# Delta attention inside a four-stage kernel: the rate products between the groups, the norm earlier, the output product between the queries, one activation table

## The reference, cut to what matters

```
xn = (x - mu) / sqrt(var + eps) * ln_w + ln_b
q, k, v = xn @ Wq.T, xn @ Wk.T, xn @ Wv.T
alpha = sigmoid(xn @ Wa.T + ba);  aR = sigmoid(xn @ WaR.T + baR)
beta  = sigmoid(xn @ Wb.T + bb);  gamma = sigmoid(xn @ Wg.T + bg)
kn = k_t / max(norm(k_t), 1e-12)
pred = S^T kn;  r = clip(v_t - pred, -1, 1)
S = a_t * S;  S = S + b_t * kn (v_t - kn S);   o  = S^T q_t
R = aR_t * R; R = R + g_t * kn (r - kn R);     o += R^T q_t
out = o @ Wo.T + residual
```

## Time and profile before

| | |
|---|---|
| time, median of 3 runs | 3872.45 us (3866.7 to 3881.83) |
| span of the profiled execution | 3870.2 us |
| TensorE matmul busy | 3279.9 us, 85% |
| TensorE weight load busy | 2481.9 us, 64% |
| VectorE busy | 2586.4 us, 67% |
| ScalarE busy | 1461.8 us, 38% |
| GpSimd busy | 942.3 us, 24% |
| ScalarE table loads of L1313 and L1371 | 32 and 31, 1283 ns each |

### The profile page before, as it was taken

How to read it: one execution, slowest core, us unless ns; L and a number is a source line. 1 busy time by engine, 2 the same in 40 slices (tenths; PEclk the granted TensorE clock), 3 DMA queues, 4 the chain that set the end, 5 groups by cost and what they waited for, 6 DMA issues and landing times. The chain is left out here.

```text
span 3870.2 us, 141857 instructions
## 1 busy us (share of the span) xinstructions
PE 3279.9 (85%) x62854; PEld 2481.9 (64%) x62854; DVE 2586.4 (67%) x5676; ACT 1461.8 (38%) x3298; POOL 942.3 (24%) x1051
## 2 busy tenths in 40 slices
PE   7775999994889988888888988888888899857888
PEld 4555999993566666666666666666666666534555
DVE  6872111212777787778777887777777877747887
ACT  2221222221454445444544454445444544421111
POOL 2333222221222222322222222222222222212110
PEclk9886999996899999999999999999999999978999
DMA  2117666662000000000000000000000000010000
GB/s 67 58 47 237 184 183 183 191 181 91 5 7 10 9 7 7 10 9 7 7 10 9 7 7 10 9 7 7 10 9 7 7 9 8 5 40 18 22 24 14
DMA packets 98175, 168.18 MB, mean 43 GB/s; under 512 B 15400, under 2 KB 71976, under 8 KB 97312
## 3 DMA queue, kind: packets, MB, share of 16 engines
q1 hardware_dynamic: 76976, 136.07, 10.6%
q0 software_dynamic: 19440, 21.97, 4.0%
q10 hardware_dynamic: 1152, 1.06, 0.1%
HBM read 118.86 MB, written 38.09 MB: 41 GB/s over the span
## 5 line engine op out<-in xcount | busy, mean ns | idle before, releaser
L1357 ACT COPY da_Ub<-da_U 32x256 f32<-32x256 f32 x1024 | 412.0, 402 | 17.1
L1051 POOL TENSOR_TENSOR da_M<-da_M,da_decay 128x512 f32<-128x512 f32 x256 | 283.4, 1131 | 456.9 <-DVE da_M L1212 322.7
L1189 DVE TENSOR_TENSOR da_eGn<-da_eGn,da_z 128x30 f32<-128x30 f32 (+14 forms) x960 | 353.6, 368 | 33.0
L1188 DVE TENSOR_TENSOR da_z<-da_eGn 128x30 f32<-128x30 f32 (+14 forms) x960 | 349.5, 364 | 27.6
L1644 PE MATMUL da_C<-da_Ub,da_Km 128*64 128x256 f32 x2048 | 313.4, 426 | 16.1 <-ACT da_Ub L1357 5.7
L829 PEld LDWEIGHTS le_ps_qkv<-le_scr,le_up 128*128 128x128 f32 x2272 | 266.0, 193 | 4.8 <-ACT le_scr L659 1.8
L829 PE MATMUL le_ps_qkv<-le_scr,le_up 128*128 128x128 f32 x2272 | 268.0, 277 | 1.2 <-ACT le_scr L659 1.2
L1476 PE MATMUL da_unit<-da_wx,da_xnT 128*128 128x512 f32 x512 | 258.1, 629 | 2.9 <-ACT da_xnT L1302 1.9
L1483 PE MATMUL da_unit<-da_xnT,da_wx 128*128 128x128 f32 x2048 | 244.4, 278 | 10.6 <-ACT da_eGn L1342 10.5
L1212 DVE TENSOR_TENSOR da_M<-da_C,da_M 128x512 f32<-128x512 f32 x256 | 176.5, 689 | 113.9 <-PE da_C L1644 108.2
L1483 PEld LDWEIGHTS da_unit<-da_xnT,da_wx 128*128 128x128 f32 x2048 | 235.7, 193 | 18.2 <-ACT da_eGn L1342 18.2
(11 more groups left out here) (303 smaller groups left out, 7105.3 us busy)
## 6 DMA issues: line engine op xcount, KB each, us to landing
le_up<-in_upT SPq DMA_DIRECT2D x71, 1024.0 KB, 5.1
le_scr<-moe_slots SPq DMA_DIRECT2D x71, 129.0 KB, 4.2
le_down<-in_downT SPq DMA_DIRECT2D x8, 1024.0 KB, 12.4
le_x<-in_x SPq DMA_DIRECT2D x16, 256.0 KB, 3.6
moe_acc<-le_y SPq DMA_DIRECT2D x32, 128.0 KB, 2.3
da_x<-moe_acc SPq DMA_DIRECT2D x128, 32.0 KB, 1.9
stream<-da_xz SPq DMA_DIRECT2D x128, 32.0 KB, 1.6
stream<-da_y POOLq DMA_DIRECT2D x128, 32.0 KB, 3.0
```

Of the source, the lines that this page charges most:

```text
L1051: ins = nc.gpsimd.tensor_tensor(st_, st_, decay[:, par, rec, 2 * g:2 * g + 2].rearrange("p a b -> p (a b)").unsqueeze(2).to_broadcast([P, ...
L1188: c.link(tt(t, Xm[:, s + 1:C, s:s + 1].to_broadcast([P, below, s]), Xm[:, s:s + 1, 0:s].to_broadcast([P, below, s]), ALU.mult))
L1189: c.link(tt(Xm[:, s + 1:C, 0:s], Xm[:, s + 1:C, 0:s], t, ALU.add))
L1357: ins = nc.scalar.copy(Ub[rows_of(b), :, :, b, :], U[rows_of(b), rec])
```

## The change

- `exponents_next` and its semaphore are gone. ScalarE loads one table with exponential and logarithm at the stage's start.
- TensorE: `turn_x` goes behind the state rows of group 1, `rates` 0 ahead of the first Gram product, `rates` 1 to where `result` was, `rates` 2 behind the state rows of group 3, `rates` 3 ahead of the predicted product of group 3. `result` goes between the two halves of the queries. `turned_outputs` 0 goes behind the second token product of group 2 (`state_update(i, 2, 0)`), `turned_outputs` 1 between the inner outputs. `turned_keys` 1 and the first half of the values go ahead of `state_update(i, 3, 0)`, `turned_keys` 2 ahead of the last inner outputs.
- VectorE: `norm_second` goes ahead of `clipped` 0, `norm_last` ahead of the gates, the four `add_bias` into groups 1, 1, 2 and 3.
- ScalarE: the copy of x, the exponentials and the logarithms are spread over groups 0 to 3 in the same way; each logarithm is by itself.
- The banks of `rates` and `turned_outputs` and the waits that guard them change with it.

No product, copy or elementwise step is added; only the small exponential of L1371 is left out.

```diff
-        RATE_BANK = (2, 0, 1, 2)
+        RATE_BANK = (0, 2, 1, 2)
+        OUT_BANK = (2, 0, 0, 0)
...
@@ VectorE, period @@
                     products(n, pn, 0, 1)
+                if norm:
+                    norm_second(i + 2)
                 if state:
                     clipped(i, par, 0)
...
                     update(i, 0, 0)
                 if norm:
-                    norm_second(i + 2)
+                    norm_last(i + 2)
                 if prepare:
                     gates(n)
...
                     products(n, pn, 1, 1)
+                if norm:
+                    add_bias(i + 2, 0)
+                if prepare:
                     gram_out(n, pn, 2)
...
                     update(i, 1, 1)
+                if norm:
+                    add_bias(i + 2, 1)
                 if prepare:
                     gram_out(n, pn, 3)
                     decays(pn, 0)
                     decays(pn, 1)
-                if norm:
-                    norm_last(i + 2)
...
                     update(i, 2, 1)
+                if norm:
+                    add_bias(i + 2, 2)
                 if prepare:
                     substitute(6, 11)
                 if state:
                     clipped(i, par, 3)
                 if norm:
-                    add_bias(i + 2, 0)
-                    add_bias(i + 2, 1)
+                    add_bias(i + 2, 3)
@@ ScalarE @@
-            def exponents_next(n):
-                need(act, warmed, n)
-                nc.scalar.activation(spare[:], mhalf[:], ACT.Exp).then_inc(warmed, 1)
...
                     queries(n, 0)
+                if put:
+                    result(i - 1)
+                if prepare:
                     queries(n, 1)
...
                 if norm:
                     copy_xT(i + 2, par)
                 if state:
+                    solved(i, 1, 0)
+                if norm:
+                    rate_exp(i + 2, 0)
+                if state:
+                    solved(i, 1, 1)
+                    outputs(i, 1)
+                if norm:
+                    rate_exp(i + 2, 1)
+                    rate_log(i + 2, 0)
+                if state:
+                    solved(i, 2, 0)
+                    turned_outputs(i, 0)
+                    solved(i, 2, 1)
+                    turned_outputs(i, 1)
+                    outputs(i, 2)
+                if prepare:
+                    turned_keys(n, 0)
+                if norm:
+                    rate_exp(i + 2, 2)
+                if state:
                     turned_outputs(i, 2)
                     solved(i, 3, 0)
+                if prepare:
+                    turned_keys(n, 1)
                 if norm:
-                    for u in range(3):
-                        rate_exp(i + 2, u)
+                    rate_exp(i + 2, 3)
+                if prepare:
+                    values(n, 0)
                 if state:
                     solved(i, 3, 1)
                 if norm:
-                    rate_exp(i + 2, 3)
...
+                    rate_log(i + 2, 1)
+                if prepare:
+                    turned_keys(n, 2)
                 if state:
                     outputs(i, 3)
                 if prepare:
                     values(n, 1)
-                    turned_keys(n, 2)
-                if norm:
-                    exponents_next(i + 1)
 
             act.wait_ge(loaded, 16 * LOADS)
+            nc.scalar.preload_act_table_set("natural_log_exp_and_others")
@@ TensorE, rates @@
                     need(pe, xT_ready, n + 1)
-                    need(pe, km_ready, (n - 1) * NG + 1)
+                    need(pe, g_ready, (n - 1) * 6 + 6)
                 elif u == 1:
-                    need(pe, oT_ready, (n - 2) * NG + 3)
-                elif u == 3:
-                    need(pe, a_ready, n * 4 + 1)
+                    need(pe, gram_done, once(n - 1, 0))
+                elif u == 2:
+                    need(pe, gram_done, once(n - 1, 3))
+                else:
+                    need(pe, a_ready, n * 4 + 2)
+                    need(pe, km_ready, once(n - 1, 0))
@@ TensorE, gram @@
                     if k == 1:
                         need(pe, g_ready, n * 6 + 6)
-                        need(pe, out_ready, n - 1)
-                    elif k == 2:
-                        need(pe, oT_ready, (n - 1) * NG + 1)
+                    if k < 3 and exists(n + 1):
+                        need(pe, a_ready, (n + 1) * 4 + k)
@@ TensorE, period @@
                     queries(n, pn, 0)
+                if put:
+                    result(i - 1)
+                if prepare:
                     queries(n, pn, 1)
...
                     state_rows(i, par, 1)
+                if norm:
+                    turn_x(i + 2)
+                if state:
                     state_update(i, 0, 1)
                     state_predicted(i, par, 1)
                     solve(i, 1, 0)
                     state_outputs(i, par, 1)
+                if norm:
+                    rates(i + 2, par, 0)
                 if prepare:
                     gram(n, pn, 2)
                 if state:
                     inner_predicted(i, par, 1)
                     state_update(i, 1, 0)
-                if put:
-                    result(i - 1)
+                if norm:
+                    rates(i + 2, par, 1)
                 if state:
                     solve(i, 1, 1)
                     inner_outputs(i, par, 1, 0)
                 if prepare:
                     gram(n, pn, 3)
                 if state:
-                    turned_outputs(i, 0)
...
                     state_update(i, 2, 0)
-                    turned_outputs(i, 1)
+                    turned_outputs(i, 0)
                     solve(i, 2, 1)
                     inner_outputs(i, par, 2, 0)
+                    turned_outputs(i, 1)
                     inner_outputs(i, par, 2, 1)
                     state_rows(i, par, 3)
+                if norm:
+                    rates(i + 2, par, 2)
                 if prepare:
                     turned_keys(n, 0)
...
-                if norm:
-                    turn_x(i + 2)
-                if state:
                     turned_outputs(i, 2)
                     solve(i, 3, 0)
                     state_outputs(i, par, 3)
                 if norm:
-                    rates(i + 2, par, 0)
+                    rates(i + 2, par, 3)
                 if state:
                     inner_predicted(i, par, 3)
-                if norm:
-                    rates(i + 2, par, 1)
+                if prepare:
+                    turned_keys(n, 1)
+                    values(n, pn, 0)
                 if state:
                     state_update(i, 3, 0)
-                if norm:
-                    rates(i + 2, par, 2)
-                if state:
                     solve(i, 3, 1)
                     inner_outputs(i, par, 3, 0)
-                if norm:
-                    rates(i + 2, par, 3)
-                if prepare:
-                    turned_keys(n, 1)
-                    values(n, pn, 0)
+                if prepare:
+                    turned_keys(n, 2)
                 if state:
                     inner_outputs(i, par, 3, 1)
```

More of the change, by code:

```diff
@@ L942, in chunked_delta @@
          tt_ready, chain, pool_chain, cleared, w_psum, w_ready, u_psum, u_ready, ub_ready, p_psum, wr_ready, ds_psum, s_updated, dr_psum, r_updated,
-         o_psum, o_ready, scaled, oT_psum, oT_ready, out_psum, out_ready, added, warmed) = [m.sem(n) for n in names]
+         o_psum, o_ready, scaled, oT_psum, oT_ready, out_psum, out_ready, added) = [m.sem(n) for n in names]
         sq = eG[:, 1, 0:DI].rearrange("p (h t) -> p h t", t=P)
@@ L1308, in rate_exp, with rate_log @@
                 nc.scalar.activation(a, a, ACT.Exp, scale=-1.0).then_inc(e_done, 1)
-            def rate_log(n):
-                for rec in range(2):
-                    need(act, e_done, n * 4 + 2 * rec + 2)
-                    nc.scalar.activation(sp[:, rec], sp[:, rec], ACT.Ln, bias=1.0).then_inc(sp_ready, 1)
+            def rate_log(n, rec):
+                need(act, e_done, n * 4 + 2 * rec + 2)
+                nc.scalar.activation(sp[:, rec], sp[:, rec], ACT.Ln, bias=1.0).then_inc(sp_ready, 1)
             def keys(n, half):
@@ L1405, in period @@
                     outputs(i, 0)
-                    solved(i, 1, 0)
-                if put:
-                    result(i - 1)
-                if state:
-                    solved(i, 1, 1)
-                    turned_outputs(i, 0)
-                    outputs(i, 1)
-                    solved(i, 2, 0)
-                    turned_outputs(i, 1)
-                    solved(i, 2, 1)
-                if prepare:
-                    turned_keys(n, 0)
-                if state:
-                    outputs(i, 2)
                 if norm:
@@ L1460, in turn_x @@
                 need(pe, xn_ready, n + 1)
-                need(pe, gram_done, once(n - 1, 3))
+                need(pe, g_ready, (n - 1) * 6 + 5)
```

(43 more changed lines are left out.)

20 lines of the change are left out of this document (6 added, 14 removed).

## The result

The changed kernel takes 3742.16 us (median of 4 runs, 3736.06 to 3752.39) where the kernel before takes 3877.14 in the same comparison: a ratio of 0.9658, 95% interval 0.9639 to 0.9677. It is faster by 3.4%, 135 us; 3759 was predicted. The profiled execution spans 3742.7 us, 127.5 less than that of before.

The account below looks back on a forecast made before the run. TensorE was taken as the bound. Removed waits of 3.7 us, less 1.4 new, plus 1.3 clock, gave 3.6 a period over 30 periods; with start and end 113 us off 3870.2, plus 2.3: 3759 us, range 3675 to 3835.

Parts of the forecast that it names:

- The bound and the ledger of waits: Delta stage, steady part: TensorE bounds the 77.8 us period, idle 9.5, of which 4.65 are listed waits for other engines.
- One table, 1.1: ScalarE before the outputs' turn and the keys: without the second table load and small exponential, 1.1 of 1.16 us a period go.
- The 2.6 us for the start: Ahead of the first period: two table switches of 1.28 us that nothing hides, saved once.
- Rates 0 under the wait for the keys' product, 1.2: TensorE before the first Gram product: rates 0 fills the wait for VectorE, saving 1.2 of 1.41 us a period.
- Values and bias, 1.1: TensorE's waits for the values' copy, 0.85 us a period, and for the rates' bias, 0.25, all go.
- W of group 3, 0.3: Before group 3's solve: rates 2 gives VectorE 1.9 us to bring W, saving 0.3 of 0.68 us a period.
- The output product, 0: Moved between the queries' halves on TensorE, with rates 1 in its old place: cost moved, not changed, 0 us.
- New waits, 1.4: Norms, bias adds, exponentials and logarithm put ahead of other work on VectorE and ScalarE: 1.4 us a period lost, bounds 0 to 5.8.
- Clock, 1.3: TensorE's granted clock: rates 0 fills the idle time after which it fell, 1.3 of 3.1 us a period back.
- Gaps that take the gain: Rival, TensorE's short matmuls: waits turn into "issue" gaps, about 1 us a period added, clock term 0; 3828 us, chance 0.18.
- Loads that stay: Rival, ScalarE: table loads remain at each exponential-logarithm switch, four a period in place of two; 3838 us, chance 0.04.
- The ring of ScalarE, VectorE and TensorE: Rival, slower: exponentials, bias adds and copies of U wait on each other, 1.5 us per coupling; 3936 us, chance 0.08.

## Why the prediction was right, by its steps

3759 us was forecast and 3742 measured; per period 3.6 us less and 4.22. That the two are so near is in part luck: one step had no price for what it rests on, and two terms were off by 0.7 us in opposite ways.

- **The bound and the ledger of waits.** Right. Nearly all the gain lies in rows and in the clock; the time ahead of the stage and behind it changed by 0.4 and 1.3 us.
- **One table, 1.1.** Right in the changed kernel (0.91 gone, the 0.28 stays), wrong as a term by itself: alone it gives 0.29. The prediction asked what is late next only on ScalarE and TensorE's own growth product, not at the next place where TensorE meets VectorE, 8 us later. The 2.6 us for the start don't show in the changed kernel: the first turn of the triangle (L1194, later L1195) starts at 1001.7 us before and at 1002.3 after.
- **Rates 0 under the wait for the keys' product, 1.2.** Measured 1.31 of wait gone; putting rates 0 behind the Gram product costs 1.02 and brings 0.73 of the wait back, so the filler is not all of it.
- **Values and bias, 1.1.** Gone, 1.13. The reason given was distance between the halves on TensorE. No run moved them apart alone. What a run shows is that the copy first, without a shorter tail on ScalarE, only hands the wait to the copy of the outputs.
- **W of group 3, 0.3.** 0.62: of 0.66 there are 0.04 left. But W of group 0 now costs 0.25, at the period's first solve, which the prediction had no term for.
- **The output product, 0.** This is the step that failed in its reason. The cost of the product is indeed only moved, but the prediction named as cover for it "VectorE is still in its substitution" and priced the place at nothing. That end is what TensorE meets first: without the product in front of it the kernel waits 3.64 us there and is at 1.0192, which is more than all the other savings together. And the product with the table, without the other edits, gives no more than the table (0.9951 for 0.9956); the product alone was not run. The gain is that of the set, and the terms of the sum are no prices of single edits.
- **New waits, 1.4.** Mis-sized: 0.67 (W of group 0 0.24, U 0.15, norms of the keys 0.14, W of rec 1 0.13, Gram copy 0.01). Small waits of 0.34 and pauses of 0.16 that I had not counted went, and the gaps have 0.16 more. Where I put 0.4 on the bias add ahead of the Gram copy, nothing came; the exponential and the logarithm ahead of `solved` 2 leave no row at all.
- **Clock, 1.3.** Mis-sized: 0.6. Its mechanism isn't borne out for rates 0 either: with 0.73 of the wait back the low time did not rise, in one profile.
- The two mis-sizings, +0.7 and -0.7, 0.3 more on the waits that went and 0.3 on the small ones make the 4.2 for 3.6.
- **Rivals.** Gaps that take the gain: they stayed (3.95 and 4.11). Loads that stay: priced at 2.6 us a period, 1.45 when tried. The ring of ScalarE, VectorE and TensorE that would make it slower: its couplings cost 0.1 to 0.3 us here, under the 0.9 from which it decides. VectorE's chain across the period's border can bound the kernel all the same: with the product back it shows as 3.64 us.

## What to carry to other kernels

When three engines of one pipeline are each near busy, a wait that goes lets the next one appear at the next meeting point: trace for each removed wait where the engine then arrives, for a whole period, and look there for the other engine's last instruction. Long independent work of the bounding engine did most here ahead of the instruction that ends the other engine's longest unbroken run: the same product is worth 6.85 us a period in the changed kernel, and nothing measurable in the kernel before with one table, where other waits stand next. And a run of short instructions has a cost of its own at the borders of the list's blocks: with long ones spread through it the gaps fell by 0.66 to 0.95 us a period, of which half came back as other waits.

## What the runs showed of the hardware

- TensorE's gaps without a releaser fall at one place modulo 256 of its list, 404 of 405 in three kernels, and cost 3.95 us of a period of 77.66. The block ahead of such a gap, gap included, lasted 3.6 us on the median in the kernel before. A long block in front can spare a short one the gap (19 of 42 behind blocks of 4.5 us or more, 4 of 77 behind shorter ones).
- With sixty-four instructions more ahead of a stage of some 115000 the time was 0.4 to 0.5% less, in two runs. Differences of this size between two orders of the same work are not to be read as worth of the order; the 0.45% of the two spread rates is one of them.
- The clock fell most where TensorE had waited longest: 15.8 us a period at 1.2 GHz with a wait of 3.64 us for VectorE, 5.18 in the changed kernel, 3.30 in two of the versions with rates spread. That a given wait is the cause was not tested apart, and the kernel with rates 0 behind the Gram product speaks against so simple a rule (0.73 us more of one wait, 0.35 less of low clock).
- Some of VectorE's 128x512 products double in length beside GpSimd's scaling of the state, 0.69 to 1.53 us, as in the earlier trace rows: 39 of 448 in the kernel before and 12 in the changed one last over 1.1 us, and none where the output product is back in group 1. No run took it away alone, so its price stays open.
